# Multiplying the scan states of a pair by C in one VectorE instruction of 1024 elements instead of two of 512

## The chip, the cores and the metric

The kernel runs on one core of a Trainium2 chip. The metric is the device time of one execution in microseconds, as the median of several runs. All arithmetic is in float32.

## The reference, cut to what matters

The model is a chain of eight stages over x (8 x 512 x 256): self attention, cross attention, a gated feed forward, four state-space layers ("mamba"), a norm, and three more attention and feed-forward stages. The change lies in the four state-space layers, which compute:

```python
xdbl = jnp.einsum('bsd,fd->bsf', xi, xp_w)
dt, Bm, Cm = jnp.split(xdbl, [DR_, DR_ + DS_], axis=-1)
dt = jax.nn.softplus(jnp.einsum('bsr,er->bse', dt, dtp_w) + dtp_b)
A = -jnp.exp(A_log)
dA = jnp.exp(dt[..., None] * A)
dBu = dt[..., None] * Bm[:, :, None, :] * xi[..., None]
# for every time step, with h the state of 512 channels x 16:
h = da * h + dbu
y = jnp.einsum('bes,bs->be', h, c)
# after the scan:
y = (y + xi * Dp) * jax.nn.silu(z)
```

So each channel has 16 states, every state is a first-order recurrence in time, and the outputs are the states times C, summed over the 16 states.

## The kernel before, in words

Stages run one after another with a barrier between them. In the `mamba` stage the 8 sequences of 576 steps are one line of 4608 columns, cut into 9 chunks of 512 columns. A **body** is one chunk of one layer; there are 4 x 9 = 36 bodies, written as a loop of two rounds of 18.

A body has 64 **units** (i = 0 to 63) of 128 partitions x 512 time steps, in 32 **pairs** (pair j holds units 2j and 2j+1). For each unit:

- ScalarE (ACT) writes exp(dt x A) into one of four PSUM banks (L2474). The banks are `slot_of(i)`, two pairs deep, so pair j uses the banks of pair j-2. Before it may, `slots_free` (L2123 to L2134) waits until pair j-2 is done with them (semaphore `prod_d` for VectorE's pairs, L2132), copies the last column of both banks out as the state for the next body (L2133, 128x2), and waits for that copy.
- GpSimd (POOL) writes u x B for both units of a pair into a ring of six pair buffers (L2506), in one instruction of 1024 elements.
- VectorE (DVE) runs the recurrence (L2429, `tensor_tensor_scan`), which waits for both.
- The state is multiplied by C. BY_POOL names 10 of the 32 pairs (0, 5, 8, 11, 14, 16, 20, 24, 26, 28): their scans write into the ring and POOL multiplies the pair (L2511), three pairs later, once ACT's copy of the last column (L2129, semaphore `kept`) has been made. For the other 22 pairs the scan stays in PSUM, and VectorE multiplies it into the ring (`times_c`, L2237), which then raises `prod_d`.
- TensorE (PE) sums the pair into a bank of y (L2384, four matmuls of 64 output rows each in the trace), which frees the ring buffer.

Each engine has its own program, written by hand in a fixed order. Beside the pairs they carry the projections of the next chunk at fixed places. Those of ACT count here: after exp 7 the silu of z (L2168, with a table load before and after, L2168 and L2169), after exp 13 the copy of the fourth block of x, which waits for PE (L2161, PE's L1992 with `E3` in `late_pe`), after exp 15 the silu of x (L2173, L2174), after exp 37 and exp 45 the softplus of two blocks of dt (L2185, L2119, L2121, L2187). VectorE also gates y with silu(z) before scans 7, 23, 39 and 55 (L2232) and scales the norm before scans 26 and 27 (L2222).

The order on VectorE before the change is scan 2j, second product of pair j-1, scan 2j+1, first product of pair j.

Of the kernel before, what the change touches and what calls it, by code (L numbers as in the profile page):

```python
# [18 lines left out]
ALU = mybir.AluOpType  # L19
# [3 lines left out]
P = 128  # L23
# [1708 lines left out]
TC = 512  # L1732
# [6 lines left out]
SP_ = DS // 2  # L1739
# [132 lines left out]
def val(N, per, off):  # L1872

    l, j = N
    return l * (BODIES * per) + (j * per + off)
# [14 lines left out]
def v_at(N, name):  # L1890

    return BEFORE_V[name] + 1 if N[1] == -2 else val(N, len(LANE_V), V_BASE + LANE_V[name] + 1)


def s_at(N, name):

    return BEFORE_S[name] + 1 if N[1] == -2 else val(N, len(LANE_S), S_BASE + LANE_S[name] + 1)
# [12 lines left out]
def mamba(core):  # L1910
# [17 lines left out]
    bc = core.weights[0][:, 0:SP_ * 2 * TC].rearrange("p (a c t) -> p a c t", a=SP_, c=2)  # L1928
# [6 lines left out]
    banks = core.banks  # L1935
# [17 lines left out]
    da_full, fed, scanned, prod_d, prod_q, summed = S("da_full"), S("fed"), S("scanned"), S("prod_d"), S("prod_q"), S("summed")  # L1953
# [3 lines left out]
    by_pool = lambda j: j % SP_ in BY_POOL[j // SP_]  # L1957
    d_index = lambda j: sum(not by_pool(i) for i in range(j))
    q_index = lambda j: sum(by_pool(i) for i in range(j))
    slot_of = lambda i: 2 * (i // 2 % 2) + i % 2  # L1960
    da_full_at = lambda N, i: val(N, UN, i + 1)
    fed_at = lambda N, j: val(N, PAIRS_N, j + 2)
    scanned_at = lambda N, i: val(N, UN, i + 1)
# [12 lines left out]
    ring_pair = lambda n, j: ring[:, (n * PAIRS_N + j) % RING]  # L1976
# [239 lines left out]
    def early_dve(e, N, i, c, nb):  # L2216

        if i == SCALE_AT:
            e.wait_ge(rstd, val(N, 2, 6))
        if i in (SCALE_AT, SCALE_AT + 1):  # L2220
            k = i - SCALE_AT
            last = e.scalar_tensor_tensor(out=nb[:, k, TAPS - 1:], in0=chunk(c + 2)[:, k, :], scalar=lv("norm", k), in1=lane_v,  # L2222
                                          op0=ALU.mult, op1=ALU.mult)
            if k == 1:
                last.then_inc(ln.v_free, 1)

    def gate(e, N, k, zi):

        e.wait_ge(summed, summed_at(N, SP_ * (k + 1) - 1))
        if k == 0:  # L2230
            e.wait_ge(silu, val(N, 2, 3))
        e.tensor_tensor(zi[:, k, :], ybank[k % 2], zi[:, k, :], ALU.mult).then_inc(gated, 1)  # L2232

    def times_c(e, N, n, j, h):

        i = 2 * j + h
        last = e.tensor_tensor(ring_pair(n, j)[:, h, :], banks[:, slot_of(i), :], bc[:, j % SP_, 1, :], ALU.mult)  # L2237
        if h == 1:
            last.then_inc(prod_d, 1)

    def next_decay_act(e):
        e.activation(decay_next, layer_vec(core, "A_log", "A_log"), ACT.Exp).then_inc(decay_exp, 1)
# [42 lines left out]
    with core.nc.Block() as block:  # L2285
# [107 lines left out]
        @block.vector  # L2393
        def _(e):
            e.memset(state, 0.0).then_inc(set_up, 1)
            e.memset(scrap[:, 18:22], 0.0)
            e.memset(far, FAR).then_inc(set_up, 1)
            e.memset(tiny, TINY).then_inc(set_up, 1)
            e.tensor_tensor(fold, core.ident[:, 0:64], core.ident[:, 64:128], ALU.add).then_inc(set_up, 1)
            e.memset(scrap[:, 1:2], 0.0).then_inc(prod_d, 1)  # L2400
            e.memset(scrap[:, 2:3], 0.0).then_inc(prod_d, 1)
            e.memset(scrap[:, 3:4], 0.0).then_inc(gated, 1)
            for i in range(RING - 1):
                e.memset(scrap[:, 4 + i:5 + i], 0.0).then_inc(summed, 1)
            e.wait_ge(core.first_loaded, FIRST_LOAD)
            for i in range(UN):
                early_dve(e, (0, -2), i, -2, normed[:, 0])
            for i in range(UN):
                early_dve(e, (0, -1), i, -1, normed[:, 1])
            for l in range(LAYERS // 2):  # L2410
                for n in range(BODIES):
                    N, c = (l, n), n % CHUNKS
                    layer = l * 2 + n // CHUNKS
                    for i in range(UN):
                        j, h = i // 2, i % 2
                        k, a = j // SP_, j % SP_
                        if c == CHUNKS - 2 and i == SCALE_AT:
                            e.wait_ge(core.first_loaded, layer * FIRST_LOAD + 2 * FIRST_LOAD)
                        early_dve(e, N, i, c, normed[:, n % 2])
                        for f in range(KI - 1):  # L2420
                            if i == 16 * (f + 1) + 7:
                                gate(e, N, f, z[:, n % 2])
                        if i == 7:
                            gate(e, previous(N), KI - 1, z[:, (n + 1) % 2])
                        if h == 0:
                            e.wait_ge(fed, fed_at(N, j))
                        e.wait_ge(da_full, da_full_at(N, i))
                        da, ub = banks[:, slot_of(i), :], ring_pair(n, j)[:, h, :]
                        e.tensor_tensor_scan(ub if by_pool(j) else da, da, ub, state[:, i:i + 1], ALU.mult, ALU.add).then_inc(scanned, 1)  # L2429
                        if h == 0 and j > 0 and not by_pool(j - 1):  # L2430
                            e.wait_ge(scanned, scanned_at(N, i - 1))
                            times_c(e, N, n, j - 1, 1)
                        if h == 1 and not by_pool(j):
                            e.wait_ge(scanned, scanned_at(N, i - 1))
                            times_c(e, N, n, j, 0)
                        if h == 1 and j == PAIRS_N - 1 and not by_pool(j):
                            e.wait_ge(scanned, scanned_at(N, i))
                            times_c(e, N, n, j, 1)
            N = (LAYERS // 2, 0)
            gate(e, previous(N), KI - 1, z[:, (BODIES - 1) % 2])  # L2440
            for m in range(KD):
                e.wait_ge((ln.s_full, ln.v_full)[m], (s_at(previous(N), "E2"), v_at(previous(N), "E1"))[m] + 1)
                xc = chunk(CHUNKS - 1)[:, m, :]
                e.tensor_tensor(xc, xc, lanes[1 - m], ALU.add)
# [384 lines left out]
```

## Time and profile before

| | us |
|---|---|
| median of 3 runs | 6634.21 (6632.14 to 6638.02) |
| the profiled execution: own time | 6639.8 |
| its span, first to last instruction | 6638.0 |
| VectorE busy | 4928.1 (74%) |
| TensorE matmul busy | 6129.0 (92%) |
| GpSimd busy | 4394.1 (66%) |
| ScalarE busy | 3620.5 (55%) |
| first scan to last scan of the mamba stage | 2054.0 to 5992.7 |

Busy times are the durations of an engine's instructions, with overlaps of neighbours counted once. A timeline gives the start of an instruction, its duration, and in brackets how long the engine had been idle before it and on what it had waited. A duration runs over the start of the next instruction of the same engine, so what an instruction costs its engine is the distance from its start to the next start, which is called its **step** below.

### The profile page before, as it was taken

Reading aid. Unit: us, or ns where it says so; the run is one execution under the profiler, and the core shown is the slowest. Engines: PE = TensorE matmul, PEld = TensorE weight load, DVE = VectorE, ACT = ScalarE, POOL = GpSimd, SP = SyncE. Lnnn points to the kernel's source line nnn. Section 1 sums busy time; section 2 is a strip of 40 time slices with the busy share of each in tenths; the row PEclk is TensorE's granted clock in tenths of the full one; section 3 lists DMA queues with packets and bytes.
Section 4 is the critical chain, followed back from the end, with each engine's and each line's share of the span. In section 5 each row is a group of like instructions: output and inputs, shape, how many; then the busy total and the mean of one; then the engine's idle time right before and its main releaser. Section 6 shows DMA issues by size and latency. Waiting matters only on the chain. (4 is left out here: it accounts for less than half of the span.)

```text
span 6638.0 us, 60681 instructions
## 1 busy us (share of the span) xinstructions
PE 6129.0 (92%) x20586; PEld 2577.4 (39%) x20586; DVE 4928.1 (74%) x5709; ACT 3620.5 (55%) x6605; POOL 4394.1 (66%) x2056
## 2 busy tenths in 40 slices
PE   9999999999999989898899989898989898988898
PEld 4555555544443333323333323333323343323444
DVE  4444445543225999999999999999999999995623
ACT  4444445432225666666666666666666666664432
POOL 3333334323005999999999999999999999992300
PEclk9999999999998989899989999999999898989998
DMA  2000000213002333333333333332333232332000
GB/s 80 1 1 1 1 1 1 86 26 102 20 0 68 83 76 78 78 93 85 72 89 71 83 88 86 71 89 65 89 81 93 65 89 65 93 80 56 4 0 26
DMA packets 228678, 387.64 MB, mean 58 GB/s; under 512 B 46304, under 2 KB 64416, under 8 KB 225936
## 3 DMA queue, kind: packets, MB, share of 16 engines
q1 hardware_dynamic: 228368, 383.75, 23.7%
q8 instruction: 164, 2.69, 0.2%
q14 instruction: 146, 1.20, 0.1%
HBM read 207.14 MB, written 23.40 MB: 35 GB/s over the span
## 5 line engine op out<-in xcount | busy, mean ns | idle before, releaser
L2506 POOL TENSOR_TENSOR work<-work,weights 128x1024 f32<-128x1024 f32 x1152 | 2685.6, 2361 | 15.8 <-PE banks L2384 6.8
L2429 DVE TENSOR_TENSOR_SCAN banks<-banks,work 128x512 f32<-128x512 f32 x1584 | 1985.7, 1272 | 53.5 <-ACT banks L2474 48.1
L2384 PE MATMUL banks<-work 128*64 128x512 f32 x4608 | 1353.9, 670 | 378.2 <-POOL work L2511 271.1
L2474 ACT ACTIVATE banks<-work 128x512 f32<-128x512 f32 x2304 | 1496.0, 680 | 25.5
L1992 PE MATMUL banks<-work,weights 128*128 128x512 f32 (+31 forms) x3796 | 1140.6, 451 | 3.0 <-DVE work L2222 3.0
L2237 DVE TENSOR_TENSOR work<-banks,weights 128x512 f32<-128x512 f32 x1584 | 1056.0, 668 | 0.0
L2511 POOL TENSOR_TENSOR work<-work,weights 128x1024 f32<-128x1024 f32 x360 | 848.0, 2356 | 238.4 <-ACT work L2129 238.4
L2429 DVE TENSOR_TENSOR_SCAN work<-banks,work 128x512 f32<-128x512 f32 x720 | 911.2, 1269 | 99.8 <-ACT banks L2474 97.2
L603 POOL TENSOR_TENSOR work<-work 128x1024 f32<-128x1024 f32 x256 | 479.6, 1893 | 743.4 <-DVE work L470 742.9
L1992 PEld LDWEIGHTS banks<-work,weights 128*128 128x128 f32 x3796 | 634.4, 190 | 600.0 <-issue 523.6
L2133 ACT ACTIVATE work<-banks 128x2 f32<-128x2 f32 x792 | 135.9, 172 | 1227.4 <-DVE work L2237 1225.6
L2384 PEld LDWEIGHTS banks<-work 128*64 128x64 f32 x4608 | 271.0, 145 | 1236.4 <-issue 500.8
L553 ACT ACTIVATE work<-banks,work 128x512 f32<-128x512 f32 x512 | 347.7, 690 | 201.1 <-DVE work L464 201.1
L464 DVE TENSOR_REDUCE work<-banks 128x2 f32<-128x1024 f32 x256 | 308.8, 1214 | 105.1 <-PE banks L389 104.7
L2010 PE MATMUL banks<-work,weights 128*128 128x512 f32 x592 | 350.7, 722 | 0.0
L1040 PE MATMUL banks<-work,weights 128*128 128x512 f32 x768 | 341.5, 599 | 9.4 <-ACT work L215 9.4
L454 DVE COPY work<-banks 128x512 f32<-128x512 f32 x256 | 175.5, 685 | 160.3 <-PE banks L379 160.3
L379 PE MATMUL banks<-ident,work 128*128 128x128 f32 x2048 | 277.9, 279 | 8.2 <-DVE work L454 4.6
L379 PEld LDWEIGHTS banks<-ident,work 128*128 128x128 f32 x2048 | 222.1, 141 | 151.7 <-issue 111.1
L389 PE MATMUL banks<-work 64*128 64x512 f32 x1024 | 254.4, 615 | 0.0
L366 PE MATMUL banks<-work 128*64 128x256 f32 x2048 | 247.5, 385 | 0.0
L322 PE MATMUL banks<-work,weights 128*128 128x512 f32 x512 | 224.9, 597 | 6.4 <-ACT work L215 4.2
(312 smaller groups left out, 6796.9 us busy)
## 6 DMA issues: line engine op xcount, KB each, us to landing
weights<-mamba_bc SPq DMA_DIRECT2D x592, 256.0 KB, 5.0
work<-work SPq DMA_DIRECT2D x1160, 128.0 KB, 2.3
weights<-mamba_taps SPq DMA_DIRECT2D x5, 2048.0 KB, 7.5
weights<-cross_vo SPq DMA_DIRECT2D x16, 512.0 KB, 6.9
mamba_taps<-work SPq DMA_DIRECT2D x4, 2048.0 KB, 7.8
cross_vo<-weights SPq DMA_DIRECT2D x6, 1024.0 KB, 8.4
work<-in_conv_rows SPq DMA_DIRECT2D x16, 256.0 KB, 6.7
out_T<-X SPq DMA_DIRECT2D x8, 512.0 KB, 3.3
```

The source lines that it names most:

```text
L379: mm = e.transpose(core.banks[:, 4 + j, kt * P:(kt + 1) * P], probs[:, 2 * (g % 2) + u, j, kt * P:(kt + 1) * P], core.ident[:])
L553: last = e.activation(probs[:, slot, j, :], core.banks[:, 2 * u + j, :], ACT.Exp, bias=nmax[:, slot, j:j + 1], accum_out=sums[:, slot, j:j ...
L603: e.tensor_tensor(probs[:, slot], probs[:, slot], rsum[:, slot, :].unsqueeze(2).to_broadcast([P, 2, T]), ALU.mult) \
L1040: mm = e.matmul(bank(i), w1[:, k, m * P:(m + 1) * P], normed[:, k, :], start=(k == 0), stop=(k == KD - 1))
L1992: mm = e.matmul(lane[:, a:b], conv_w[j][:, k, m * P:(m + 1) * P], nb[:, k, a + j:b + j], start=(d == 0 and k == 0), stop=(j == 0 and b == ...
L2010: mm = e.matmul(lane, z_w[:, k, m * P:(m + 1) * P], nb[:, k, TAPS - 1:], start=(k == 0), stop=(k == KD - 1))
L2237: last = e.tensor_tensor(ring_pair(n, j)[:, h, :], banks[:, slot_of(i), :], bc[:, j % SP_, 1, :], ALU.mult)
L2384: mm = e.matmul(ybank[k % 2][64 * h:64 * h + 64, :], fold, ring_pair(n, j)[:, h, :], start=False, stop=(a == SP_ - 1))
L2429: e.tensor_tensor_scan(ub if by_pool(j) else da, da, ub, state[:, i:i + 1], ALU.mult, ALU.add).then_inc(scanned, 1)
L2474: e.activation(banks[:, slot_of(i), :], dt_rep[:, k % 2, h, :], ACT.Exp, scale=decay[:, f:f + 1]).then_inc(da_full, 1)
L2506: e.tensor_tensor(ring_pair(n, j), u_rep[:, k % 2], bc[:, a, 0, :].unsqueeze(1).to_broadcast([P, 2, TC]), ALU.mult) \
L2511: e.tensor_tensor(ring_pair(n, q), ring_pair(n, q), bc[:, q % SP_, 1, :].unsqueeze(1).to_broadcast([P, 2, TC]), ALU.mult) \
```

## The change

`times_c` takes both units of the pair at once: one product of 128 x 1024 over two PSUM banks, with C broadcast over the units. It is issued where the second product stood, behind the first scan of the next pair (for the last pair of a body behind its own second scan), and the place behind the second scan of the pair becomes empty. The scan, the waits of the other engines and what they count stay as they are.

```diff
-    def times_c(e, N, n, j, h):
-
-        i = 2 * j + h
-        last = e.tensor_tensor(ring_pair(n, j)[:, h, :], banks[:, slot_of(i), :], bc[:, j % SP_, 1, :], ALU.mult)
-        if h == 1:
-            last.then_inc(prod_d, 1)
+    def times_c(e, N, n, j):
+
+        e.wait_ge(scanned, scanned_at(N, 2 * j + 1))
+        e.tensor_tensor(ring_pair(n, j), banks[:, slot_of(2 * j):slot_of(2 * j) + 2, :], bc[:, j % SP_, 1, :].unsqueeze(1).to_broadcast([P, 2, TC]), ALU.mult) \
+            .then_inc(prod_d, 1)
...
                         if h == 0 and j > 0 and not by_pool(j - 1):
-                            e.wait_ge(scanned, scanned_at(N, i - 1))
-                            times_c(e, N, n, j - 1, 1)
-                        if h == 1 and not by_pool(j):
-                            e.wait_ge(scanned, scanned_at(N, i - 1))
-                            times_c(e, N, n, j, 0)
+                            times_c(e, N, n, j - 1)
                         if h == 1 and j == PAIRS_N - 1 and not by_pool(j):
-                            e.wait_ge(scanned, scanned_at(N, i))
-                            times_c(e, N, n, j, 1)
+                            times_c(e, N, n, j)
```

The instructions of VectorE around scans 6 to 10 of a body (pairs 3 to 5) before. L2429 is the scan, L2237 the product with C, L2232 the gating of y:

```order
L2429 SCALAR_TENSOR_TENSOR banks<-banks,work 128x512 [waits mamba_da_full,mamba_fed]
L2237 TENSOR_TENSOR work<-banks,weights 128x512 [waits mamba_scanned]
L2232 TENSOR_TENSOR work<-banks,work 128x512 [waits mamba_summed]
L2429 SCALAR_TENSOR_TENSOR banks<-banks,work 128x512 [waits mamba_da_full]
L2237 TENSOR_TENSOR work<-banks,weights 128x512 [waits mamba_scanned]
L2429 SCALAR_TENSOR_TENSOR banks<-banks,work 128x512 [waits mamba_da_full,mamba_fed]
L2237 TENSOR_TENSOR work<-banks,weights 128x512 [waits mamba_scanned]
L2429 SCALAR_TENSOR_TENSOR banks<-banks,work 128x512 [waits mamba_da_full]
L2237 TENSOR_TENSOR work<-banks,weights 128x512 [waits mamba_scanned]
L2429 SCALAR_TENSOR_TENSOR work<-banks,work 128x512 [waits mamba_da_full,mamba_fed]
```

The same scans 6 to 10 now (the scan is L2428):

```order
L2428 SCALAR_TENSOR_TENSOR banks<-banks,work 128x512 [waits mamba_da_full,mamba_fed]
L2237 TENSOR_TENSOR work<-banks,weights 128x1024 [waits mamba_scanned]
L2232 TENSOR_TENSOR work<-banks,work 128x512 [waits mamba_summed]
L2428 SCALAR_TENSOR_TENSOR banks<-banks,work 128x512 [waits mamba_da_full]
L2428 SCALAR_TENSOR_TENSOR banks<-banks,work 128x512 [waits mamba_da_full,mamba_fed]
L2237 TENSOR_TENSOR work<-banks,weights 128x1024 [waits mamba_scanned]
L2428 SCALAR_TENSOR_TENSOR banks<-banks,work 128x512 [waits mamba_da_full]
L2428 SCALAR_TENSOR_TENSOR work<-banks,work 128x512 [waits mamba_da_full,mamba_fed]
```

Between scan 7 and scan 8, where a product of 512 stood, nothing is left; all of pair 3's product stands behind scan 8.

The end of a body on VectorE before (scan 63, both products of pair 31, scan 0 of the next body):

```order
L2429 SCALAR_TENSOR_TENSOR banks<-banks,work 128x512 [waits mamba_da_full]
L2237 TENSOR_TENSOR work<-banks,weights 128x512 [waits mamba_scanned] x2
L2429 SCALAR_TENSOR_TENSOR work<-banks,work 128x512 [waits mamba_da_full,mamba_fed]
```

And now:

```order
L2428 SCALAR_TENSOR_TENSOR banks<-banks,work 128x512 [waits mamba_da_full]
L2237 TENSOR_TENSOR work<-banks,weights 128x1024 [waits mamba_scanned]
L2428 SCALAR_TENSOR_TENSOR work<-banks,work 128x512 [waits mamba_da_full,mamba_fed]
```

Here the one product waits for the scan directly in front of it. The programs of ACT, POOL and PE are the same as before.

## Rows read from the trace of the kernel before

**Rows 1.** The page: span, and the busy tenths of an engine in 40 slices.

```profile
span 6638.0 us, 60681 instructions
...
DVE  4444445543225999999999999999999999995623
...
POOL 3333334323005999999999999999999999992300
```

**Rows 2.** Busy time by stretch: all 36 bodies, and one body.

```profile
core 0: us, PE busy (x) PEld busy (x) DVE busy (x) ACT busy (x) POOL busy (x), PEclk, DMA share, GB/s
2054.00:5995.00 3941.00, 3562.79 (x10575) 1301.65 (x10574) 3809.31 (x4104) 2535.20 (x4505) 3684.90 (x1662) 0.92 0.35 81
3262.10:3371.00 108.90, 98.73 (x305) 39.26 (x304) 105.74 (x115) 70.38 (x125) 102.40 (x47) 0.91 0.34 78
```

**Rows 3.** Groups of instructions, 2054 to 5995 us: count, busy us, mean ns, idle before.

```profile
L2429 DVE TENSOR_TENSOR_SCAN banks<-banks,work 128x512 f32<-128x512 f32 x1584 | 1985.7, 1272 | 53.5 <-ACT banks L2474 48.1 <-issue 1.0
...
L2237 DVE TENSOR_TENSOR work<-banks,weights 128x512 f32<-128x512 f32 x1584 | 1056.0, 668 | 0.0
L2429 DVE TENSOR_TENSOR_SCAN work<-banks,work 128x512 f32<-128x512 f32 x720 | 911.2, 1269 | 99.8 <-ACT banks L2474 97.2 <-POOL work L2506 2.6
```

**Rows 4.** Timeline of DVE, body from 3262.09 on: scans 2 to 4, 8 and 16.

```profile
3264.46 2.44 DVE L2429 TENSOR_TENSOR_SCAN banks<-banks,work 128x512 f32<-128x512 f32 x2
3266.81 0.67 DVE L2237 TENSOR_TENSOR work<-banks,weights 128x512 f32<-128x512 f32 x1
3267.40 1.27 DVE L2429 TENSOR_TENSOR_SCAN banks<-banks,work 128x512 f32<-128x512 f32 x1
3268.59 0.67 DVE L2237 TENSOR_TENSOR work<-banks,weights 128x512 f32<-128x512 f32 x1
...
3274.52 0.67 DVE L2237 TENSOR_TENSOR work<-banks,weights 128x512 f32<-128x512 f32 x1
3276.33 1.29 DVE L2429 TENSOR_TENSOR_SCAN banks<-banks,work 128x512 f32<-128x512 f32 x1 [1.14 <-ACT banks L2474]
...
3288.76 0.67 DVE L2237 TENSOR_TENSOR work<-banks,weights 128x512 f32<-128x512 f32 x1
3291.34 1.28 DVE L2429 TENSOR_TENSOR_SCAN work<-banks,work 128x512 f32<-128x512 f32 x1 [1.91 <-ACT banks L2474]
```

**Rows 5.** Timeline of ACT, same body: before and behind the first silu block, and L2161.

```profile
3269.29 0.17 ACT L2133 ACTIVATE work<-banks 128x2 f32<-128x2 f32 x1 [2.00 <-DVE work L2237]
3269.49 1.30 ACT L2474 ACTIVATE banks<-work 128x512 f32<-128x512 f32 x2
...
3275.33 0.17 ACT L2133 ACTIVATE work<-banks 128x2 f32<-128x2 f32 x1
...
3283.83 0.69 ACT L2161 ACTIVATE work<-banks,weights 128x512 f32<-128x512 f32 x1 [0.55 <-PE banks L1992]
```

**Rows 6.** Timeline of DVE, same body, the first softplus place (scan 38).

```profile
3326.95 0.67 DVE L2237 TENSOR_TENSOR work<-banks,weights 128x512 f32<-128x512 f32 x1
3327.67 1.29 DVE L2429 TENSOR_TENSOR_SCAN banks<-banks,work 128x512 f32<-128x512 f32 x1
```

**Rows 7.** Timeline of DVE, the end of the same body.

```profile
3368.64 1.27 DVE L2429 TENSOR_TENSOR_SCAN banks<-banks,work 128x512 f32<-128x512 f32 x1
3369.82 1.26 DVE L2237 TENSOR_TENSOR work<-banks,weights 128x512 f32<-128x512 f32 x2
3371.01 2.44 DVE L2429 TENSOR_TENSOR_SCAN work<-banks,work 128x512 f32<-128x512 f32 x2
```

**Rows 8.** Timeline of DVE in cross attention: 1024-element instructions that read PSUM.

```profile
1307.89 1.22 DVE L892 TENSOR_REDUCE work<-banks 128x16 f32<-128x1024 f32 x1 [3.79 <-PE banks L848]
1309.15 1.22 DVE L896 TENSOR_TENSOR work<-banks,work 128x1024 f32<-128x1024 f32 x1
1310.29 1.27 DVE L870 TENSOR_TENSOR work<-X,banks 128x512 f32<-128x512 f32 x2
```

**Rows 9.** Timeline of POOL and then PE, same body: the last waits before the next body.

```profile
3335.43 2.35 POOL L2511 TENSOR_TENSOR work<-work,weights 128x1024 f32<-128x1024 f32 x1 [1.00 <-ACT work L2129]
...
3358.92 1.08 PE L2384 MATMUL banks<-work 128*64 128x512 f32 x4 [0.52 <-POOL work L2511]
```

## The prediction, made before the changed kernel was run

> **What bounds the kernel now.** I read the page first: VectorE and GpSimd are in the nineties from about 2054 to 5993 us, in the state-space stage, and only there [rows 1]. The windows narrow it down: over all 36 bodies VectorE is busy 3809 of 3941 us (97%), GpSimd 3685, TensorE 3563, ScalarE 2535, and an ordinary body takes 108.90 us with VectorE busy 105.74 [rows 2]. So VectorE sets the pace. The groups say what it does: 2304 scans of 1.27 us, 1584 products of 668 ns, and 153.3 us of idle time ahead of scans, 145.3 of it waiting for ScalarE's exp [rows 3].
>
> Durations overlap here, so I count steps (start to start). Two scans in a row take 2.35 from the first start to the next instruction, 1.175 each; a scan behind a product takes 1.19 (3267.40 to 3268.59); a product takes 0.59 though it lasts 0.67 [rows 4]. So an instruction ends 0.08 after its successor starts.
>
> Where VectorE waits is fixed by ScalarE. Each body has four places at which a block with two table loads stands between one exp and the next: ahead of scans 8 and 16 (1.14 and 1.91 us of idle [rows 4]) and of scans 38 and 46 (step 0.72 where 0.59 is needed, so 0.13 [rows 6]; scan 46 repeats it). At each of the four the last thing VectorE does before it waits is a first product: 0.59 us of useful work inside the wait.
>
> **The change, part by part.**
>
> *The merged product.* 792 pairs have two steps of 0.59, 1.18 together; now they have one step t of 1024 elements. The nearest row is L896, the same operation on as many elements, one operand in PSUM, one in SBUF: it lasts 1.22 and its step is 1.14 (1309.15 to 1310.29) [rows 8]. That is the upper value. For the lower one, let the merge also save the 0.08 by which a product outlasts its step: 1.18 - 0.08 = 1.10 [rows 4]. I take t = 1.13, near L896. Against it stands a rule of the Trainium skill, "VectorE: DVE Perf Modes", in the section on the TRN2 errata: an instruction with a PSUM source costs 120 cycles at 0.96 GHz beside its elements, a large tile pays that once and many small tiles pay it each time. By that rule a pair saves 125 ns, 792 pairs 99 us, and the run would take 6535 us. The rows show that most of such a start-up is already covered by the neighbour, since 0.59 and not 0.67 is the step.
>
> *The scans.* Now scan 2j+1 and scan 2j+2 follow each other, so one of the two is of the 1.175 kind. A pair takes 1.19 + 1.175 + t where it took 2 x (1.19 + 0.59) = 3.56. It gains g = 1.195 - t = 0.065 us.
>
> *The four places.* The product's work cannot fill the wait any more: behind scan 7 nothing is left to do until exp 8 is there, and the whole product, t, comes after scan 8 where only 0.59 came. Each place costs t - 0.59 = 0.54 us behind the wait. ScalarE's block is not shortened: it starts from the release of an earlier pair, at the product's end, which moves by less than 0.1.
>
> *Release and next exp.* A product's end at 3269.26 (3268.59 + 0.67) [rows 4] lets ScalarE copy at 3269.29 [rows 5]. From a copy to the scan it leads to is 1.00 (3275.33 [rows 5] to 3276.33 [rows 4]). So the scan can start 1.03 after the product's end. Now one scan stands between (it starts 0.08 before that end and takes 1.19), so VectorE is there after 1.11. It fits, with 0.08 to spare where it had 0.67 (a product's step more was between): no cost, but a thin cover.
>
> *End of the body.* Scan 63 to scan 0 takes 2.37 [rows 7]. Now the product waits for the scan itself. The reduce at 1307.89 lasts 1.22 and the L896 that waits for it starts 1.26 later [rows 8], so 0.04 past its end: 1.27 + 0.04 + 1.13 = 2.44, a loss of 0.07.
>
> *The sum of a body, along VectorE and ScalarE.* From scan 16 to the next scan 16, gains count only where no ScalarE block decides the time. They are 13 of 22 pairs: 9, 10, 12, 13, 15 up to the release that starts the block of scan 38; 19 up to that of scan 46; 23, 25, 27, 29, 30; 1 and 4 in the next body. The others lie beside a block (or are one of the four places). So 4 x 0.54 + 0.07 - 13 x 0.065 = +1.38 us. But part of the way was slack: ScalarE's copy at 3283.83 between scans 13 and 14 had waited 0.55 for TensorE [rows 5], so a delay up to there is absorbed for 0.55. That leaves +0.83.
>
> *The other chain.* TensorE's own time for that copy comes down from GpSimd: its last wait of the body is at 3335.43 for the copy behind scan 41, and from there it runs without a gap into the next body; TensorE's last wait is for GpSimd at 3358.92 [rows 9]. Between scan 16 and scan 41 lie two places (the products behind scan 16 and scan 38) and 6 gains: 2 x 0.54 - 6 x 0.065 = +0.69. The body takes the longer of the two, +0.83.
>
> Over 36 bodies that is +30 us. The profiled execution took 6639.8 (span 6638.0), 5.6 above the median; the same sum on it gives 6670, on the median of 6634.2 it gives 6664. With t = 1.14 a body loses 2.20 + 0.08 - 0.72 - 0.55 = 1.01 (+36 us), with t = 1.10 the other chain decides, 1.02 - 0.57 = 0.45 (+16 us). Some bodies wait longer for TensorE, and there 0.69 holds, so I take 6662.
>
> The change's other sides cost nothing: 792 instructions and as many waits fewer on VectorE count only in its steps; TensorE and the ring see `prod_d` at the same point of the order; GpSimd, 102.40 of 108.90 busy [rows 2], gets more room.
>
> **The rivals.**
>
> *A. The merge saves more, and the sides cancel.* The durations speak for it: 2 x 0.668 [rows 3] against 1.22 [rows 8] is 0.11. If all of that came off the step, t = 1.07: the chain of VectorE and ScalarE gives 4 x 0.48 + 0.01 - 13 x 0.125 - 0.55, below zero, the other 2 x 0.48 - 6 x 0.125 = +0.21, in all +8 us: 6642. Against it: L896's own step of 1.14. The Trainium skill's 120 cycles (same page and section), put into the same two chains, come out here too: t = 1.055 and +0.09 a body, an estimate of 6637 from that page; its 6535 needs B besides, and has a hundredth of the chance at most.
>
> *B. Faster: the waits at the four places do not grow.* This needs ScalarE's blocks to begin 0.54 us sooner, as they would if ScalarE ran ahead instead of waiting for each release. Then only the gains are left, and the chain over GpSimd decides: -6 x 0.065 = -0.39 a body, -14 us, 6620. It decides from the point where t - 0.59 times two falls under 6 x (1.195 - t), that is t below 1.04. Against it: ahead of the block ScalarE had waited 2.00 us for the release [rows 5], so it starts from it.
>
> *C. Slower still: the 0.08 of cover is not there.* If the merged product's end, or the copy of its two banks, comes 0.13 later than its step says, each of the 13 pairs waits 0.05: 13 x 0.05 x 36 = +23 more, 6687.
>
> *D. TensorE's slack is not there,* since its work moves along with VectorE's: +1.38 a body, +50, 6684.
>
> **How the numbers follow.** A measurement of this kernel tells about 0.2%, 13 us, from no change. The forecast gets 0.62, C and D 0.16 together, all slower: 0.78. A gets 0.15, the same. B gets 0.07, faster. The range reaches down over A to 6634 and up over D and most of C to 6690.
>
> **What would show it.** The product's step, start to start, at 1.10 to 1.14. The idle time ahead of scans 8, 16, 38 and 46 each longer: 0.5 to 0.7 more at 8, 38 and 46, less at 16 if TensorE's slack went (ScalarE's wait ahead of L2161 near zero). Ahead of other scans no wait. The step from scan 63 to scan 0 about 2.44. A body of 109.7. I would be wrong if idle time ahead of every VectorE scan 2j appeared (C), if the four places stayed at 1.14, 1.91, 0.13 and 0.13 (B), or if t were under 1.08 (A).

## The result, and the profile after

The changed kernel takes 6664.26 us (median of 6 runs), the kernel before 6637.00 in six runs beside it: a ratio of 1.0041, 95% interval 1.0026 to 1.0056. It is slower by 27 us. Two of the six runs of the changed kernel took 10167 and 15655 us and are left out of the ratio; the other four lie between 6662.35 and 6664.91.

The page of the changed kernel and its windows, to be held against [rows 1, 2]:

```profile
span 6661.5 us, 59889 instructions
...
PE 6129.8 (92%) x20586; PEld 2571.2 (39%) x20586; DVE 4882.9 (73%) x4917; ACT 3620.4 (54%) x6605; POOL 4395.8 (66%) x2056
```

```profile
core 0: us, PE busy (x) PEld busy (x) DVE busy (x) ACT busy (x) POOL busy (x), PEclk, DMA share, GB/s
2053.00:6021.00 3968.00, 3564.71 (x10579) 1299.35 (x10577) 3762.22 (x3312) 2534.38 (x4506) 3686.09 (x1662) 0.92 0.35 81
3270.10:3379.70 109.60, 99.49 (x306) 39.20 (x306) 104.42 (x93) 70.31 (x126) 102.37 (x47) 0.91 0.34 78
```

VectorE has 47 us less to do in the state-space stage (3762 for 3809), and the stage is 26 us longer from first to last scan. So the stage holds all of the loss, as near as the runs can tell. The ordinary body went from 108.9 to 109.6 us.

The groups of VectorE in that stage, against [rows 3]:

```profile
L2428 DVE TENSOR_TENSOR_SCAN banks<-banks,work 128x512 f32<-128x512 f32 x1584 | 1959.0, 1271 | 124.0 <-ACT banks L2468 123.6 <-issue 0.4
L2237 DVE TENSOR_TENSOR work<-banks,weights 128x1024 f32<-128x1024 f32 x792 | 952.2, 1202 | 1.2
L2428 DVE TENSOR_TENSOR_SCAN work<-banks,work 128x512 f32<-128x512 f32 x720 | 908.9, 1267 | 100.9 <-ACT banks L2468 98.9 <-POOL work L2500 1.6 <-issue 0.5
```

The merged product lasts 1.202 us. The idle time ahead of scans rose from 153.3 to 224.9 us, and all but a few us of it still waits for ScalarE's exp. The 792 products gained something, and the wait took it and more.

The timeline of VectorE in the twelfth body (the one of [rows 4, 6, 7]), scans 6 to 9, 16, 37 to 38 and 63:

```profile
3277.10 2.45 DVE L2428 TENSOR_TENSOR_SCAN banks<-banks,work 128x512 f32<-128x512 f32 x2
3279.47 1.20 DVE L2237 TENSOR_TENSOR work<-banks,weights 128x1024 f32<-128x1024 f32 x1
3280.59 0.68 DVE L2232 TENSOR_TENSOR work<-banks,work 128x512 f32<-128x512 f32 x1
3281.18 1.28 DVE L2428 TENSOR_TENSOR_SCAN banks<-banks,work 128x512 f32<-128x512 f32 x1
3284.26 1.29 DVE L2428 TENSOR_TENSOR_SCAN banks<-banks,work 128x512 f32<-128x512 f32 x1 [1.79 <-ACT banks L2468]
3285.46 1.20 DVE L2237 TENSOR_TENSOR work<-banks,weights 128x1024 f32<-128x1024 f32 x1
3286.58 1.28 DVE L2428 TENSOR_TENSOR_SCAN banks<-banks,work 128x512 f32<-128x512 f32 x1
...
3299.10 1.28 DVE L2428 TENSOR_TENSOR_SCAN work<-banks,work 128x512 f32<-128x512 f32 x1 [1.93 <-ACT banks L2468]
...
3333.64 1.28 DVE L2428 TENSOR_TENSOR_SCAN banks<-banks,work 128x512 f32<-128x512 f32 x1
3335.62 1.29 DVE L2428 TENSOR_TENSOR_SCAN banks<-banks,work 128x512 f32<-128x512 f32 x1 [0.71 <-ACT banks L2468]
...
3377.25 1.28 DVE L2428 TENSOR_TENSOR_SCAN banks<-banks,work 128x512 f32<-128x512 f32 x1
3378.57 1.23 DVE L2237 TENSOR_TENSOR work<-banks,weights 128x1024 f32<-128x1024 f32 x1
3379.71 2.45 DVE L2428 TENSOR_TENSOR_SCAN work<-banks,work 128x512 f32<-128x512 f32 x2
```

How to read it: the product's step is 1.12 (3285.46 to 3286.58). Ahead of scan 8 the idle time is 1.79 where it was 1.14 [rows 4]. Ahead of scan 38 it is 0.71 where it was 0.05 (3326.95 + 0.67 to 3327.67 [rows 6]; the 0.13 of the prediction was counted on the step, and on the step it is 0.80 now); scan 46 is like it. Behind the wait stands a whole product: from scan 8 (3284.26) to scan 9 (3286.58) it is 2.32 us. Before, it was 1.79, from 3276.33 [rows 4] to the start of scan 9:

```profile
3278.12 1.28 DVE L2429 TENSOR_TENSOR_SCAN banks<-banks,work 128x512 f32<-128x512 f32 x1
```

Ahead of scan 16 the idle time hardly moved, 1.93 for 1.91 [rows 4]. Two things nearly cancel there: the first product of 0.59 no longer fills the wait, and ScalarE's block no longer starts late by the 0.55 us for which its copy L2161 had waited (next rows). From scan 63 to the next scan 0 it is 2.46 (3377.25 to 3379.71), 2.37 before [rows 7].

ScalarE in the same body, against [rows 5]:

```profile
3278.74 1.28 ACT L2168 ACT_TABLE_LOAD   x1
3280.04 1.91 ACT L2168 ACTIVATE work<-work 128x2048 f32<-128x2048 f32 x1
3281.97 1.28 ACT L2169 ACT_TABLE_LOAD   x1
3283.26 0.17 ACT L2133 ACTIVATE work<-banks 128x2 f32<-128x2 f32 x1
3283.47 1.30 ACT L2468 ACTIVATE banks<-work 128x512 f32<-128x512 f32 x2
...
3291.62 0.67 ACT L2161 ACTIVATE work<-banks,weights 128x512 f32<-128x512 f32 x1
```

The block of table load, silu and table load fills 3278.74 to 3283.26, and there is nothing between scan 7 (it ends at 3282.46) and scan 8 at 3284.26. L2161 stands without a bracket: the 0.55 us that it had waited for TensorE are gone. Over the stage its wait fell from 35.2 us at 36 of its instructions to this:

```profile
L2161 ACT ACTIVATE work<-banks,weights x37: 664/667/688, 2019.8 to 5932.7; 128x512 f32<-128x512 f32 x37
its engine sat idle before it (us, times) until:
  PE banks L1992: 16.4, 8
```

### The profile page after: what moved, and what is told of

It is laid out like the page before. It is cut to its first block and busy times, and to the rows that moved or that the text cites. A ratio compares the mean times of both kernels' runs of the same rounds, so it can differ in the third digit from the quotient of the medians.

```text
span 6661.5 us, 59889 instructions
## 1 busy us (share of the span) xinstructions
PE 6129.8 (92%) x20586; PEld 2571.2 (39%) x20586; DVE 4882.9 (73%) x4917; ACT 3620.4 (54%) x6605; POOL 4395.8 (66%) x2056
## 5 line engine op out<-in xcount | busy, mean ns | idle before, releaser
L2428 DVE TENSOR_TENSOR_SCAN banks<-banks,work 128x512 f32<-128x512 f32 x1584 | 1959.0, 1271 | 124.0 <-ACT banks L2468 123.6
L2428 DVE TENSOR_TENSOR_SCAN work<-banks,work 128x512 f32<-128x512 f32 x720 | 908.9, 1267 | 100.9 <-ACT banks L2468 98.9
L2237 DVE TENSOR_TENSOR work<-banks,weights 128x1024 f32<-128x1024 f32 x792 | 952.2, 1202 | 1.2
```

Of the source, the lines that this page charges most:

```text
L2237: e.tensor_tensor(ring_pair(n, j), banks[:, slot_of(2 * j):slot_of(2 * j) + 2, :], bc[:, j % SP_, 1, :].unsqueeze(1).to_broadcast([P, 2, T ...
```

## The experiments

The theory after the result was that of the prediction: the product costs nothing by itself, what costs are the places at which a first product used to fill ScalarE's wait, and two chains share the loss. The rival was that the merged product costs something at each pair, through its later release or its two banks.

All kernels have the same scans and the same programs on the other engines. They differ by two tables: which of VectorE's pairs are merged, and which have their product early, behind their own second scan (the other merged pairs have it behind the next scan). A pair that is not merged and not early keeps its two products where they were in the kernel before.

```diff
+MERGED = ...
+EARLY = ...
...
+                        if h == 0 and j > 0 and not by_pool(j - 1) and j - 1 not in EARLY:
+                            if j - 1 in MERGED:
+                                times_c_pair(e, N, n, j - 1)
+                            else:
+                                times_c(e, N, n, j - 1, 1)
+                        if h == 1 and not by_pool(j):
+                            own = j in EARLY or j == PAIRS_N - 1
+                            if j not in MERGED:
+                                times_c(e, N, n, j, 0)
+                                if own:
+                                    times_c(e, N, n, j, 1)
+                            elif own:
+                                times_c_pair(e, N, n, j)
```

The results together. Ratios are to the kernel before, timed in the same set of runs; "body" is the twelfth body in the trace, from its scan 0 to the next (108.92 before, 109.62 for the change); "all scans" is the time from the first to the last scan less the 3938.7 us of the kernel before (the change: +26.3). Body and scans are read from one profiled execution of each kernel, and the one of the kernel before belongs to the set of the result, so for a few us the ratio decides.

| kernel | merged | early | us | ratio (95%) | body | all scans |
|---|---|---|---|---|---|---|
| split_four | all but 3, 7, 18, 22 | none | 6640.9 | 1.0008 (0.9999 to 1.0017) | 108.97 | +0.2 |
| merge_four | 3, 7, 18, 22 | none | 6687.3 | 1.0075 (1.0063 to 1.0088) | 110.42 | +50.6 |
| early_merged | all | 3, 7, 18, 22 | 6637.2 | 1.0000 (0.9991 to 1.0009) | 108.80 | -5.7 |
| early_split | none | 3, 7, 18, 22 | 6627.3 | 0.9987 (0.9978 to 0.9996) | 108.59 | -11.6 |
| merge_3 | 3 | none | 6641.1 | 0.9997 (0.9988 to 1.0006) | 108.95 | +2.5 |
| merge_7 | 7 | none | 6660.7 | 1.0026 (1.0015 to 1.0036) | 109.47 | +20.2 |
| merge_22 | 22 | none | 6640.5 | 0.9997 (0.9988 to 1.0006) | 108.97 | +1.8 |
| merge_3_22 | 3, 22 | none | 6651.2 | 1.0011 (1.0003 to 1.0020) | 109.40 | +14.1 |
| merge_9 | 9 | none | 6651.7 | 1.0018 (1.0009 to 1.0027) | 109.29 | +13.3 |
| split_five | all but 3, 7, 9, 18, 22 | none | 6628.5 | 0.9982 (0.9973 to 0.9990) | 108.61 | -10.1 |
| early_five | all | 3, 7, 9, 18, 22 | 6621.0 | 0.9970 (0.9958 to 0.9981) | 108.45 | -17.9 |
| early_three | all | 7, 9, 18 | 6621.5 | 0.9970 (0.9959 to 0.9982) | 108.45 | -17.1 |

The kernel before itself took 6635.6, 6646.2 and 6640.3 us in the three sets (rows 1 to 4, 5 to 8, 9 to 12 of the table), so the us column is to be compared within a set only.

### Where the loss sits: four kernels

```diff
+MERGED = (0, 1, 2, 4, 5, 6, 8, 9, 10, 11, 12, 13, 14, 15, 16, 17, 19, 20, 21, 23, 24, 25, 26, 27, 28, 29, 30, 31)
+EARLY = ()
```

> The product is merged for 18 of VectorE's 22 pairs; pairs 3, 7, 18 and 22, whose first product stood in the wait ahead of scans 8, 16, 38 and 46, keep their two products of 512. Theory 'places' (the loss is only that these four first products no longer fill ScalarE's wait): the loss vanishes and the gains stay, 6 of 0.07 us a body on the chain over GpSimd and TensorE, so a body of 108.5 and about 15 us under before (6622). Idle ahead of scans 8, 16, 38, 46 near that of before (1.2, 2.0, 0.15, 0.15 us). Rival 'every pair' (the merged product costs something at each pair, through its release or its two banks): 18/22 of the loss stays, 22 us over before (6659).

```diff
+MERGED = (3, 7, 18, 22)
+EARLY = ()
```

> Only pairs 3, 7, 18 and 22 have the merged product, the other 18 keep two. Theory 'places': the four losses without the gains, 4 x 0.53 less the slack of 0.55 us that ScalarE had ahead of its copy of L2161, +1.57 us a body, 57 us over before (6694), more than with all 22 merged. Rival 'every pair': 4/22 of the loss, +5 us (6642).

```diff
+MERGED = tuple(range(PAIRS_N))
+EARLY = (3, 7, 18, 22)
```

> All 22 merged, but for pairs 3, 7, 18 and 22 the product stands behind the pair's own second scan, inside ScalarE's wait, and not behind the next scan. Theory 'places': at scans 8 and 16 the wait is longer than the product, so the whole product is free (-0.59 us each against before); at 38 and 46 it delays the scan by about 0.45 and saves 0.59 behind it. With the gains the chain over VectorE is 2 to 3 us a body shorter, and the chain over GpSimd and TensorE decides: 0.59 + 0.14 + 6 x 0.07 = 1.15 us a body, 41 us under before (6596). Rival 'every pair': the position doesn't matter, as the changed kernel (6664).

```diff
+MERGED = ()
+EARLY = (3, 7, 18, 22)
```

> No merging: two products of 512 everywhere, but for pairs 3, 7, 18 and 22 both stand behind the pair's second scan, inside ScalarE's wait. Theory 'places': on the chain over GpSimd and TensorE 0.59 less at scan 16 and 0.13 less at scan 38, 0.7 us a body, 26 us under before (6611). Rival 'every pair': VectorE's work is the same, so the time is that of before (6637).

The rival is out. Four merged pairs cost 51 us, nearly twice what all 22 cost, and the other eighteen cost 5 us with an interval of -1 to +11; a cost at each pair would give 5 for the four and 22 for the eighteen. The place of a product alone, with no merging at all (early_split), is worth something too. Two of the four places of merge_four, ahead of scans 8 and 16 of the twelfth body:

```profile
3292.24 1.29 DVE L2438 TENSOR_TENSOR_SCAN banks<-banks,work 128x512 f32<-128x512 f32 x1 [1.73 <-ACT banks L2487]
...
3307.15 1.28 DVE L2438 TENSOR_TENSOR_SCAN work<-banks,work 128x512 f32<-128x512 f32 x1 [1.86 <-ACT banks L2487]
```

Here scan 8 waits as in the change, with none of the gains of the other pairs; the body is 1.50 us longer than before, where 1.57 was expected.

But the gains fell short three times. split_four gained nothing of the 15 us, early_merged at most 6 of the 41, early_split 8 to 12 of the 26. The timelines showed why. VectorE of split_four, scans 18 to 21:

```profile
3292.29 2.44 DVE L2438 TENSOR_TENSOR_SCAN banks<-banks,work 128x512 f32<-128x512 f32 x2
3295.04 1.29 DVE L2438 TENSOR_TENSOR_SCAN banks<-banks,work 128x512 f32<-128x512 f32 x1 [0.30 <-ACT banks L2487]
3296.24 1.21 DVE L2247 TENSOR_TENSOR work<-banks,weights 128x1024 f32<-128x1024 f32 x1
3297.36 1.28 DVE L2438 TENSOR_TENSOR_SCAN banks<-banks,work 128x512 f32<-128x512 f32 x1
```

and ScalarE at the same place, first in split_four, then in early_merged:

```profile
3293.66 0.60 ACT L2145 ACTIVATE X<-banks 128x512 f32<-128x512 f32 x1 [0.46 <-PE banks L2045]
...
3294.25 1.29 ACT L2487 ACTIVATE banks<-work 128x512 f32<-128x512 f32 x2
```

```profile
3292.40 0.60 ACT L2145 ACTIVATE X<-banks 128x512 f32<-128x512 f32 x1 [1.93 <-PE banks L2045]
```

Ahead of scan 20 there is a wait that neither the kernel before nor the change has. ScalarE must first copy a residual block out of PSUM (L2143 in the kernel before, L2145 here), and that block waits for TensorE. TensorE's run from its last wait in a body on into the next is fixed (the wait that follows the copy behind scan 41), so scan 20 is a fixed point as well, and pair 9, whose product stands around it, is a fifth place. The traces show the gate as a constant distance. Scan 41 of the eleventh body starts, in the kernel before and in split_four, at:

```profile
3224.69 1.27 DVE L2429 TENSOR_TENSOR_SCAN work<-banks,work 128x512 f32<-128x512 f32 x1
```

```profile
3222.65 1.27 DVE L2438 TENSOR_TENSOR_SCAN work<-banks,work 128x512 f32<-128x512 f32 x1
```

From there to the copy (3295.69 and 3293.66) it is 71.00 and 71.01 us, and in the twelfth body of every one of the ten kernels whose copy waits there it is 71.00 to 71.03. With the gate at 71.01 and 1.38 from the copy to a waiting scan 20, the body is 72.39 and what it takes from scan 20 to scan 41: 36.55 in split_four, 36.41 in early_merged, 36.22 in early_split, which gives 108.94, 108.80 and 108.61, for 108.97, 108.80 and 108.59 measured. In the kernel before it has a margin. VectorE and then ScalarE there, ahead of scan 20 (3297.25):

```profile
3296.66 0.67 DVE L2237 TENSOR_TENSOR work<-banks,weights 128x512 f32<-128x512 f32 x1
3297.25 1.28 DVE L2429 TENSOR_TENSOR_SCAN banks<-banks,work 128x512 f32<-128x512 f32 x1
```

```profile
3295.69 0.60 ACT L2143 ACTIVATE X<-banks 128x512 f32<-128x512 f32 x1 [0.46 <-PE banks L2043]
...
3296.27 1.29 ACT L2474 ACTIVATE banks<-work 128x512 f32<-128x512 f32 x2
```

Elsewhere a scan starts 0.79 to 0.80 after the start of its exp (3295.04 less 3294.25 in split_four). Here the exp starts at 3296.27, so scan 20 could have started at 3297.06 and started at 3297.25: 0.19 of margin. With it the sums close. From scan 20 to scan 41 split_four takes 36.55 us for the 36.36 of before (0.53 lost at scan 20, less five gains of 0.07), 0.19 more, which the margin just covers: a body of 108.97 for 108.92.

### Which losses are absorbed: four kernels

```diff
+MERGED = (3,)
+EARLY = ()
```

> Only pair 3 has the merged product, so only the place ahead of scan 8 loses 0.53 us. Theory 'two chains': the loss lies ahead of ScalarE's copy of L2161, which waited 0.55 us for TensorE before, so it is absorbed: no change within 3 us (6637), ScalarE's wait ahead of that copy down from 0.55 to about 0. Rival 'one chain' (VectorE's delays all add up to the end): +0.53 x 36 = +19 us (6656).

```diff
+MERGED = (7,)
+EARLY = ()
```

> Only pair 7 has the merged product: the place ahead of scan 16, which lies on both chains (behind TensorE's gate and ahead of GpSimd's last wait). Both theories: +0.53 x 36 = +19 us (6656); if it were as free as pair 3, the two-chain account is wrong.

```diff
+MERGED = (22,)
+EARLY = ()
```

> Only pair 22 has the merged product: the place ahead of scan 46, which lies behind GpSimd's last wait of the body (the copy behind scan 41). Theory 'two chains': the delay goes to the next body's scans and is absorbed by the same 0.55 us ahead of L2161: no change within 3 us (6637). Rival 'one chain': +19 us (6656).

```diff
+MERGED = (3, 22)
+EARLY = ()
```

> Pairs 3 and 22 merged together. Theory 'two chains': they share one slack of 0.55 us, so 1.06 - 0.55 = 0.51 us a body shows, +18 us (6655), though each alone costs nothing. Rival 'one chain': +38 us (6675). If each had a slack of its own: 0.

Pair 3 and pair 22 are free alone (body +0.03 and +0.05, ratios from 8 us under to 4 us over), pair 7 is not (+0.55), and 3 and 22 together cost +0.48 of the 0.51 expected. Over the whole run the last is less than the 18 us expected: 14 by the scans, and by the ratio 7, with an interval of 2 to 13. The bodies in which TensorE sets the time (over 109.5 us before) have more slack: but for the first of all, they moved by -0.15 to +0.54. The wait ahead of the copy of L2161 (L2163 here) in merge_3 and in merge_3_22, against 35.2 us at 36 before:

```profile
L2163 ACT ACTIVATE work<-banks,weights x37: 668/687/689, 2020.7 to 5910.8; 128x512 f32<-128x512 f32 x37
its engine sat idle before it (us, times) until:
  PE banks L1994: 17.0, 10
```

```profile
L2163 ACT ACTIVATE work<-banks,weights x37: 666/669/688, 2020.7 to 5921.9; 128x512 f32<-128x512 f32 x37
its engine sat idle before it (us, times) until:
  PE banks L1994: 14.0, 8
```

One delay uses up the wait, and a second finds none left. That is the shared slack of the two-chain account. Delays that all add up are out; a slack for each place is out by the body, while the ratio alone, with its lower bound of 1.0003, would barely exclude it.

### The fifth place, and a version that beats both kernels

```diff
+MERGED = (9,)
+EARLY = ()
```

> Only pair 9 has the merged product. The prediction counted pair 9 among the pairs that gain 0.07 us. Theory 'fifth place' (formed from the runs before): ScalarE's copy of L2143 between exp 19 and exp 20 waits for TensorE, so scan 20 is another fixed point; in the kernel before it comes 0.19 us after its exp is ready, since VectorE is that late. A merged pair 9 has nothing to do ahead of scan 20 and 1.12 behind it: +0.53 - 0.19 = 0.34 us a body, +12 us (6649). Rival 'as predicted' (scan 20 is an ordinary scan): a gain of 0.07 us a body, -2 us or nothing.

```diff
+MERGED = (0, 1, 2, 4, 5, 6, 8, 10, 11, 12, 13, 14, 15, 16, 17, 19, 20, 21, 23, 24, 25, 26, 27, 28, 29, 30, 31)
+EARLY = ()
```

> Merged but for pairs 3, 7, 9, 18 and 22, which keep two products of 512. Theory 'fifth place': keeping pair 9 split gives back on the chain from scan 20 round to scan 20 what kept split_four from its gain, 108.5 us a body for 108.93, 13 to 15 us under before. Rival (the gains of the merge are not there at all, or something else holds the body at 108.9): as split_four, 0 to 4 us over before.

```diff
+MERGED = tuple(range(PAIRS_N))
+EARLY = (3, 7, 9, 18, 22)
```

> All 22 merged; pairs 3, 7, 9, 18 and 22 have the product behind their own second scan, inside the wait. Theory 'fifth place': early_merged waited 1.0 us ahead of scan 20 with pair 9's product still to come; with it inside the wait the way from scan 20 to scan 41 is 1.0 us shorter, 107.8 us a body, 40 us under before (about 6597). Rival (another bound at 108.6 to 108.8, such as GpSimd or TensorE): as early_split, 8 us under before.

```diff
+MERGED = tuple(range(PAIRS_N))
+EARLY = (7, 9, 18)
```

> As early_five, but only pairs 7, 9 and 18 (those on the chain over GpSimd and TensorE) have the early product; 3 and 22 have it behind the next scan. If only that chain counts, as fast as early_five. Theory 'two chains': the chain along VectorE gets 1.1 us longer at scan 8 and about 0.7 at scan 46, more than the 1.1 us of wait that early_merged had ahead of scan 14, so 0.3 to 0.8 us a body slower than early_five (6610 to 6625).

Merging pair 9 alone costs 11 to 13 us, 0.37 a body for the 0.34 expected, though no table load is near it; the prediction had booked it as a gain. Its trace has the wait of split_four:

```profile
3299.33 2.44 DVE L2438 TENSOR_TENSOR_SCAN banks<-banks,work 128x512 f32<-128x512 f32 x2
3302.08 1.29 DVE L2438 TENSOR_TENSOR_SCAN banks<-banks,work 128x512 f32<-128x512 f32 x1 [0.31 <-ACT banks L2487]
```

split_five keeps the 17 other merges and brings their gain out at last: 12 us under before (6 to 18 by the interval), 13 to 15 expected.

early_five and early_three are the fastest: 19 us under the kernel before (0.9970, 0.9958 to 0.9981), and by the ratios, which are from different sets of runs (1.0041 for the change), about 0.7% under the change. For early_five 40 us were expected, and 8 by the rival; the result lies between them. What holds it is the next gate. Its VectorE at scans 18 to 22, then its ScalarE:

```profile
3288.65 2.44 DVE L2438 TENSOR_TENSOR_SCAN banks<-banks,work 128x512 f32<-128x512 f32 x2
3291.12 1.22 DVE L2247 TENSOR_TENSOR work<-banks,weights 128x1024 f32<-128x1024 f32 x1
3292.26 2.46 DVE L2438 TENSOR_TENSOR_SCAN banks<-banks,work 128x512 f32<-128x512 f32 x2
3295.12 1.28 DVE L2438 TENSOR_TENSOR_SCAN work<-banks,work 128x512 f32<-128x512 f32 x1 [0.40 <-ACT banks L2487]
```

```profile
3291.21 1.29 ACT L2487 ACTIVATE banks<-work 128x512 f32<-128x512 f32 x2
...
3293.55 0.66 ACT L2210 ACTIVATE banks<-banks,eps 128x512 f32<-128x512 f32 x1 [1.04 <-PE banks L2020]
```

The product of pair 9 now lies ahead of scan 20, inside the wait, and outlasts it: exp 20 starts at 3291.21, so scan 20 could have started at 3292.00 and starts at 3292.26. And scan 22 waits: the norm's logarithm (L2210) between exp 21 and exp 22 waits 1.04 us for TensorE. That wait was there before (L2208, also 1.04), without holding up scan 22. Its distance from scan 41 of the body before is as constant as the first gate's, 73.92 to 73.96 us in the twelfth body of all fourteen kernels, and here it closes the sum: 73.94 to L2210, 1.57 on to scan 22, 32.93 on to scan 41 is 108.44, for 108.45 measured. No run moved this gate, so that it is the bound is read from the traces alone. early_three is as fast as early_five (108.45 each), against the 0.3 to 0.8 us a body that I expected it to be slower: ScalarE's wait for TensorE ahead of L2163 is 66.2 us in all in early_five and 16.3 in early_three, so what pairs 3 and 22 lose is taken out of that wait, and the gates at scans 20 and 22 come at their own time in both. (Its 6621.5 us lie in the 6610 to 6625 expected of it, but only because early_five came out slower than expected.) So pairs 3 and 22 do not need the early product. Pairs 7, 9 and 18 lie between TensorE's gates and GpSimd's last wait; whether each of the three needs it was not tried. Nor was a kernel with early products at these pairs and no merging, so the 19 us are not divided between place and merging.

## Why the prediction was right

*The size.* 6662 was forecast, 6664.3 measured: 28 us on the 6634.2 of the kernel before, and 27 on the 6637.0 that it took beside the change. The profiled execution, 6670 forecast, took 6663.3. That the totals agree so closely is in part luck, see the chains below.

*The merged product.* Taken at 1.13 between bounds of 1.10 and 1.14; its step is 1.12, its duration 1.202. The step of two was 1.18 before, so merging saves 0.06 us. The Trainium skill, "VectorE: DVE Perf Modes", in the section on the TRN2 errata, charges 120 cycles, 0.125 us, for each instruction with a PSUM source, beside its elements. The duration agrees roughly, it falls by 0.134 (2 x 0.668 less 1.202), but the step does not: 0.08 of each product was hidden under its successor, and one such overlap is gone. Rival A, which took all of the duration's gain, is out by that.

*The scans.* As said, 1.175 behind a scan and 1.19 behind a product.

*The four places.* The core of the forecast, and the runs show it apart: t - 0.59 = 0.53 each (merge_7 +0.55 a body). Rival B, that the waits would not grow, is out: 1.79 for 1.14 and 0.71 for 0.05.

*Release and next exp.* The cover of 0.08 us held. The idle time ahead of other scans stayed near zero, so rival C did not happen.

*The end of the body.* +0.07 forecast, +0.09 measured.

*The two chains.* Forecast +0.83 for an ordinary body, measured +0.70. With t = 1.12 the forecast's own terms give 4 x 0.53 + 0.06 - 13 x 0.075 - 0.55 = +0.66. The slack of 0.55 was used up as foretold (merge_3, merge_22, merge_3_22 and the bracket that is gone at L2161), so D is out. The eleven bodies in which TensorE sets the time lost 0.5 to 1.3 us, on average 0.79, not the 0.69 of the other chain, and why so much was not looked into. Ordinary bodies lost less than forecast and these more, and the two errors offset each other: +26.3 in sum for the 28 forecast.

*Where it was wrong.* The step "gains count only where no ScalarE block decides the time" left out that ScalarE's copy ahead of exp 20, which waits for TensorE, is a gate too, with 0.19 us of margin before the change. It counted pair 9 as a gain, and alone that pair costs 0.37 a body (merge_9). It did not show in the changed kernel, whose VectorE comes too late for that gate, and so the total came out right. It showed as soon as the four places were repaired: every forecast of a gain in the first four experiments was too large for this reason, and that of early_five since the product of pair 9 outlasts this wait by 0.26 and scan 22 then waits 0.40.

## What to carry to other kernels

Two short instructions can be worth more than one long one when another engine's wait lies between them: look for the places at which the engine waits, and what it does last before each; a fused instruction moves that work behind the wait. Put the fused work inside the wait instead (here at 3 of 22 pairs), and only then count what fusing saves. And count a saving only between two points that nothing else holds. A gate with a small margin, such as the one ahead of scan 20, shows no idle time on the engine that sets the pace; here it stood in ScalarE's timeline of the kernel before, as 0.46 us of waiting for TensorE ahead of L2143.

## What the runs showed of the hardware

Joining two products of 512 float32 elements with a PSUM source took the sum of the durations from 1.336 to 1.202 us, but the step, start to start, only from 1.18 to 1.12. A product that waits for the scan directly in front of it started 0.04 us past that scan's end (3377.25 + 1.28 to 3378.57). The kernel before took 6635.6, 6646.2 and 6640.3 us in three sets of runs, 0.16% apart, about as much as several of the effects here.
